# Ordering the hand-over from attention to expert tiles: weight copies as DMAs, a second bank, and moved steps in the last group

## The reference

```
h = layernorm(x) * (1 + ca) + sa
q, k, v = split(h @ w_qkv.T)                 # 8 heads of 16
qp, kp = elu(q @ proj) + 1, elu(k @ proj) + 1   # 128 features a head
out = qp (kp^T v) / (qp . sum kp)            # in blocks of 32 tokens
x = x + ga * (out @ w_out.T + b_out)
h = layernorm(x) * (1 + cb) + sb
gates = softmax(h @ w_red @ wg_n.T); pick the largest of 8 experts
y = gelu(h @ w1[e] + b1[e]) @ w2[e] + b2[e]  # 128 -> 512 -> 128
x = x + gb * y * gates[e]
```

## Time and profile before

| | us |
|---|---|
| median of 3 runs | 273.75 (273.18 to 275.33) |
| the profiled execution | 273.41 |
| its span in the profile | 271.7 |
| TensorE's mean granted clock | 0.992 of full |

### The profile page before, as it was taken

The page is one execution under the profiler, slowest core; times in us unless marked ns, Lnnn a source line. Parts: engine busy times, 40 slices in busy tenths (PEclk is TensorE's granted clock), DMA queues, the critical chain, the costliest instruction groups (busy, mean ns, idle before and its releaser), DMA issues.

```text
span 271.7 us, 11509 instructions
## 1 busy us (share of the span) xinstructions
PE 246.3 (91%) x4004; PEld 182.2 (67%) x4005; DVE 223.6 (82%) x743; ACT 182.3 (67%) x479; POOL 159.2 (59%) x199
## 2 busy tenths in 40 slices
PE   7699889999999999999999887997788999999960
PEld 3354555666766757667666565777678999999950
DVE  6778899999999999999999999687974776667640
ACT  2865657787687777868777655758866766766730
POOL 4423135174188487595771857786889974455550
PEclk9999999999999999999999999999999999999996
DMA  6910001955407218031040044222466444344300
GB/s 174 259 45 2 2 4 43 307 114 155 127 33 209 82 53 250 17 102 62 2 149 16 12 154 128 110 87 80 160 185 182 131 131 132 117 113 124 114 21 0
DMA packets 21583, 28.44 MB, mean 105 GB/s; under 512 B 3343, under 2 KB 16531, under 8 KB 21536
## 3 DMA queue, kind: packets, MB, share of 16 engines
q1 hardware_dynamic: 17920, 19.26, 25.7%
q0 software_dynamic: 3296, 8.41, 8.7%
q10 hardware_dynamic: 320, 0.13, 0.2%
HBM read 15.38 MB, written 10.64 MB: 96 GB/s over the span
## 4 chain that ended last, share of the span: by engine, by line
PE 56%; DVE 13%; issue 7%; POOL 7%; DMA 3%; SPq 1%; ACT 1%; POOLq 1%; DVEq 0%; ACTq 0%
PE ps L883 14%; PE ps L956 9%; PE ps L984 8%; PE ps L847 6%; PE ps L894 6%; DVE phi L1259 5%; PE ps L908 3%; PE ps L923 2%; POOL sorted_rows L504 2%; DMA rin<-sorted_rows 2%; PE ps L916 2%; PE ps L950 2%; PE ps L935 1%; PE ps L836 1%; POOL out L569 1%
## 5 line engine op out<-in xcount | busy, mean ns | idle before, releaser
L639 ACT ACTIVATE ebuf<-ps 128x512 f32<-128x512 f32 x128 | 69.5, 595 | 29.8 <-PE ps L883 29.5
L1259 DVE SCALAR_TENSOR_TENSOR phi<-ebuf,ps 128x512 f32<-128x512 f32 x128 | 81.1, 675 | 2.6 <-ACT ebuf L639 2.5
L883 PE MATMUL ps<-qk,proj_w 64*128 64x512 f32 x384 | 62.0, 427 | 4.9 <-DVE phi L1259 4.3
L701 ACT ACTIVATE gT<-ps,b_cols 128x128 f32<-128x128 f32 x156 | 44.6, 368 | 17.1 <-PE ps L956 13.9
L984 PE MATMUL ps<-w_sb,gT 128*128 x312 | 42.2, 278 | 4.2 <-DVE y L1553 2.8
L984 PEld LDWEIGHTS ps<-w_sb,gT 128*128 128x128 f32 x312 | 37.9, 192 | 6.1 <-issue 5.9
L883 PEld LDWEIGHTS ps<-qk,proj_w 64*128 64x128 f32 x384 | 31.2, 184 | 15.8 <-issue 4.1
L569 POOL DMA_INDIRECT out<-yo,tok x27 | 27.4, 1013 | 21.5 <-DVE yo L1569 19.0
L504 POOL DMA_INDIRECT sorted_rows<-rec,pos x32 | 32.8, 1024 | 8.5 <-issue 7.5
L894 PEld LDWEIGHTS ps<-phi 128*32 128x32 f32 x2048 | 22.5, 112 | 20.4 <-issue 13.5
L894 PE MATMUL ps<-phi 128*32 128x32 f32 x2048 | 29.6, 199 | 0.2 <-ACT a_sb L652 0.2
(11 more groups left out here) (205 smaller groups left out, 421.6 us busy)
## 6 DMA issues: line engine op xcount, KB each, us to landing
rin<-sorted_rows SPq DMA_DIRECT2D x39, 192.5 KB
vbd<-vals SPq DMA_DIRECT2D x32, 68.0 KB
w1b<-in_L_ffn_w SPq DMA_DIRECT2D x4, 512.0 KB
w_sb<-in_L_ffn_w SPq DMA_DIRECT2D x8, 256.0 KB
sorted_rows<-pad_rec SPq DMA_DIRECT2D x9, 192.5 KB, 6.0
x_all<-in_L_attn_x SPq DMA_DIRECT2D x2, 256.0 KB, 3.5
w1b<-in_L_ffn_b SPq DMA_DIRECT2D x1, 512.0 KB
sorted_rows<-rec,pos POOLq DMA_INDIRECT x32, 2.9
```

What stands on the lines that cost most here:

```text
L639: nc.scalar.activation(ebuf[:, h % 2, j, :], x_ps[h % 2][:, j, :], ACT.Exp, scale=1.0 / SHRINK, bias=math.log(SHRINK) - 1.0).then_inc(s_ex ...
L701: last = nc.scalar.activation(gT[:, b, c_, :], h_ps[b][:, j, i * P:(i + 1) * P], ACT.Gelu, bias=b1_cols[:, bass.ds(e * FC + c_, 1)])
L883: last = mm(x_ps[h % 2][:, j, :], proj_w[rows, w_part, h, :], qk_of(g, part, h // HT)[rows, :], start=w_part < part, stop=w_part == part)
L1259: last = v.scalar_tensor_tensor(out=phi[:, h % 4, j, :], in0=ebuf[:, h % 2, j, :], scalar=SHRINK, in1=x_ps[h % 2][:, j, :], op0=ALU.min, o ...
```

## The change

- SP copies the weights of all 12 early slots by DMA within on-chip memory (`load_weights`), instead of POOL (4) and ACT (8). Each has its own semaphore `f_we[s]`, for which `hidden` and `add_bias` wait. The first two go ahead of the row fetches, those of 2 to 5 between them, those of 6 to 11 after them, behind a wait for the last scores.
- The early slots' second layer shared one bank (4); from slot 5 (`Y_APART`) it alternates between banks 4 and 6, and `outer(s)` then waits for the bias of slot s - 2, no longer of s - 1.
- In DVE's last step, `score_sum(5)`, `score_inverse(5)`, `norm2_stats(6)` and `norm2_moments(6)` leave their place before the last `features` and come into `last_head`.
- POOL: `norm2_inverse(6)` goes behind the residual base and the first scatter of group 5; two more of these scatters come ahead of `norm2_scale(6)`, and all four ahead of `norm2_inverse(7)`.
- PE: the scores of group 7 come ahead of the first early slot; slot 2's first and slot 1's second layer go behind `turn_h2(6)`; `outer(2)` goes ahead of `rank(6)`. The fillers go from 12 to 4.
- ACT: the copies go; `gate_exp(7)` comes ahead of `build_scale(6)`, and `gate_exp(6)` ahead of `keep_h2T(7)`.
- DVE: `add_bias(2)` goes ahead of the positions of group 6, the score of group 7 behind its positions, `scale_add(3)` and `add_bias(4)` ahead of two operations of the full table.

```diff
 SP
-            sp.wait_ge(s_early, 1)
+            def load_weights(s):
+                e = sp.value_load(exp_i[0:1, s:s + 1], min_val=0, max_val=E - 1)
+                sp.dma_start(w_early[s], w1b2[:, bass.ds(e * (F + D), F + D)]).then_inc(f_we[s], 16)
+            sp.wait_ge(s_early, 2)
...
+            sp.wait_ge(s_xb, NG - 1)
+            for s in range(2):
+                load_weights(s)
             rows = [row_of(s) for s in range(RING)]
             for i in range(RECS):
                 sp.wait_ge(s_scat[i], 16 * TG * ((EARLY_G - i + RECS - 1) // RECS))
-            for s, row in enumerate(rows):
-                fetch(s, row)
+            fetch(0, rows[0])
+            fetch(1, rows[1])
+            for s in range(2, RING):
+                load_weights(s)
+                fetch(s, rows[s])
+            sp.wait_ge(s_a, H * NG)
+            for s in range(RING, EARLY):
+                load_weights(s)
 POOL
-                    for s in range(POOL_TAKES):
-                        take_early(s)
...
-                if prev:
+                if prev and not is_last(g):
                     norm2_inverse(g - 1)
...
             residual_base(NG - 1, False)
             scatter(NG - 3, [0])
+            norm2_inverse(NG - 2)
+            scatter(NG - 3, [1])
             apart()
-            scatter(NG - 3, [1])
+            scatter(NG - 3, [2])
             norm2_scale(NG - 2, False)
+            scatter(NG - 3, [3])
             norm2_inverse(NG - 1)
-            scatter(NG - 3, [2])
-            scatter(NG - 3, [3])
             apart()
             put_early(0)
 ACT
             keep_in(4, 4)
+            gate_exp(NG - 2)
             keep_h2T(NG - 1)
-            gate_exp(NG - 2)
             gelu(3, 1)
             keep_logits(NG - 1)
+            gate_exp(NG - 1)
             build_scale(NG - 2)
-            take_early(6)
-            gate_exp(NG - 1)
             keep_in(5, 5)
 PE (outer)
-                if isinstance(s, int) and s <= EARLY:
+                if shares_y(s):
                     if s > 0:
                         pe.wait_ge(f_s, s)
                 else:
                     pe.wait_ge(f_s, s - 1)
+                if isinstance(s, int) and s == Y_APART:
+                    pe.wait_ge(s_lgs, NG)
 PE (order)
-            keep_busy(3, t_ps)
+            keep_busy(2, t_ps)
+            scores(NG - 1, H - 2)
+            keep_busy(2, t_ps)
+            apply_values(NG - 1, 0, False)
+            scores(NG - 1, H - 1)
             slot_in(0)
-            scores(NG - 1, H - 2)
-            apply_values(NG - 1, 0, False)
+            apply_values(NG - 1, 1, False)
             slot_hidden(0)
             slot_in(1)
...
             slot_hidden(1)
-            apply_values(NG - 1, 1, False)
+            project_out(NG - 1, ps[:, 6, :])
             slot_in(2)
             slot_outer(0)
-            project_out(NG - 1, ps[:, 6, :])
+            pe.wait_ge(s_on, 2 * NG)
+            turn_h2(NG - 2)
             slot_hidden(2)
             slot_in(3)
             slot_outer(1)
-            turn_h2(NG - 2)
+            gate(NG - 2)
             slot_hidden(3)
-            gate(NG - 2)
             slot_in(4)
...
             turn_h2(NG - 1, ps[:, 6, :])
+            outer(2, 2, e_2)
             pe.wait_ge(s_lgs, NG - 1)
             rank(NG - 2)
             gate(NG - 1, ps[:, 6, :])
-            outer(2, 2, e_2)
 DVE (last_head)
+                score_sum(NG - 3)
                 position_rows(NG - 3)
+                score_inverse(NG - 3, False)
...
                 normalise_out(NG - 1, 0)
+                norm2_stats(NG - 2)
                 normalise_sum(NG - 1, 1)
+                norm2_moments(NG - 2)
                 normalise_inverse(NG - 1, 1)
 DVE (after the groups)
             scale_add(1, 1, 0)
+            add_bias(2, 2)
             position_rows(NG - 2)
...
-            add_bias(2, 2)
             route_max(NG - 1)
             route_below(NG - 1)
             route_first(NG - 1)
-            score_sum(NG - 1)
-            score_inverse(NG - 1, False)
             scale_add(2, 2, 0)
             add_bias(3, 3)
...
             position_out(NG - 1)
+            score_sum(NG - 1)
+            score_inverse(NG - 1, False)
```

More of the change, by code:

```diff
@@ L59, in adaln_kernel @@
     EARLY_TILES = EARLY_G * TG
+    Y_APART = 5
     WHOLE = SLOTS // RING * RING
@@ L244, in s_bank, with y_bank, shares_y @@
             return ps[:, 5 if s_early or b % 2 == 0 else 7, 0:P]
-        def y_bank(s_early, b):
-            return ps[:, 4 if s_early or b % 2 == 0 else 6, 0:D]
+        def y_bank(shares, b):
+            return ps[:, 4 if shares or b % 2 == 0 else 6, 0:D]
+        def shares_y(s):
+            return isinstance(s, int) and s < Y_APART
         m_ps = ps[:, 7, :]
@@ L279, in adaln_kernel @@
         f_in = [sem(f"f_in{b}") for b in range(RING)]
-        f_t = sem("f_t"); f_table = sem("f_table"); f_ts = sem("f_ts"); f_w = sem("f_w"); f_wa = sem("f_wa"); f_wp = sem("f_wp"); s_apart = sem("s_apart"); f_m = sem("f_m"); f_oa = sem("f_oa"); s_early = sem("s_early"); s_th = sem("s_th"); f_h = sem("f_h"); f_g = sem("f_g")
+        f_we = [sem(f"f_we{i}") for i in range(EARLY)]
+        f_t = sem("f_t"); f_table = sem("f_table"); f_ts = sem("f_ts"); f_w = sem("f_w"); s_apart = sem("s_apart"); f_m = sem("f_m"); f_oa = sem("f_oa"); s_early = sem("s_early"); s_th = sem("s_th"); f_h = sem("f_h"); f_g = sem("f_g")
         f_y = sem("f_y"); f_yd = sem("f_yd");
@@ L756, in _ @@
             keep_a(NG - 1, H - 2, False)
+            nc.scalar.activation(warm[:, :], neg_half[:, 0:1], ACT.Gelu).then_inc(f_table, 1)
+            keep_a(NG - 1, H - 1, False)
             act.wait_ge(s_early, 2)
@@ L759, in _ @@
             keep_in(0, 0)
[L760 removed]
             keep_in(1, 1)
[L762 removed]
             gelu(0, 0)
[L764 to L766 removed]
             keep_in(2, 2)
             gelu(1, 1)
[L769 removed]
+            keep_h2T(NG - 2)
             keep_in(3, 3)
[L771 removed]
             gelu(2, 0)
@@ L960, in hidden @@
             def hidden(s, b):
-                if isinstance(s, int) and s < POOL_TAKES:
-                    pe.wait_ge(f_wp, s + 1)
-                elif isinstance(s, int) and s < EARLY:
-                    pe.wait_ge(f_wa, s + 1 - POOL_TAKES)
+                if isinstance(s, int) and s < EARLY:
+                    pe.wait_ge(f_we[s], 16)
                 else:
@@ L975, in outer @@
             def outer(s, b, e):
-                early = isinstance(s, int) and s < EARLY
-                if isinstance(s, int) and s <= EARLY:
+                if shares_y(s):
                     if s > 0:
@@ L981, in outer @@
                     pe.wait_ge(f_s, s - 1)
+                if isinstance(s, int) and s == Y_APART:
+                    pe.wait_ge(s_lgs, NG)
                 pe.wait_ge(f_g, s + 1)
                 for c_ in range(FC):
-                    last = mm(y_bank(early, b), gT[:, b % 2, c_, :], w2_sb[:, bass.ds(e * (FC * D) + c_ * D, D)],
+                    last = mm(y_bank(shares_y(s), b), gT[:, b % 2, c_, :], w2_sb[:, bass.ds(e * (FC * D) + c_ * D, D)],
                               start=(c_ == 0), stop=(c_ == FC - 1))
@@ L1499, in step @@
                         residual(g - 1)
-                    if h == 6:
+                    if h == 6 and not is_last(g):
                         if prev2:
@@ L1544, in add_bias @@
                 early = isinstance(s, int) and s < EARLY
-                if early and s < POOL_TAKES:
-                    dve.wait_ge(f_wp, s + 1)
-                elif early:
-                    dve.wait_ge(f_wa, s + 1 - POOL_TAKES)
+                if early:
+                    dve.wait_ge(f_we[s], 16)
                 else:
@@ L1552, in add_bias @@
                 w = w_early[s] if early else w_slot[b]
-                v.tensor_tensor(y1[:, b % 2, :], y_bank(early, b), w[:, F:F + D], ALU.add).then_inc(f_s, 1)
+                v.tensor_tensor(y1[:, b % 2, :], y_bank(shares_y(s), b), w[:, F:F + D], ALU.add).then_inc(f_s, 1)
             def scale_add(s, b, k):
@@ L1573, in finish @@
                 scale_add(s, b, k)
-            add_bias(0, 0)
             residual(NG - 1)
             norm2_stats(NG - 1)
+            add_bias(0, 0)
             norm2_moments(NG - 1)
@@ L1608, in _ @@
             v.tensor_scalar(last_row[:, 0:E], carry[:, :], -float(P), None, ALU.add).then_inc(s_last, 1)
+            scale_add(3, 3, 0)
+            add_bias(4, 4)
             dve.wait_ge(s_tab, 1)
@@ L1613, in _ @@
             v.tensor_reduce(nt[:, :], full[:, :, :], AX.X, ALU.add).then_inc(s_tab, 1)
-            scale_add(3, 3, 0)
-            add_bias(4, 4)
             dve.wait_ge(s_tab, 3)
```

38 lines of the change are left out of this document (5 added, 33 removed).

## The result

The changed kernel takes **278.95 us** (median of 4 executions, 278.75 to 283.32; the record lists a fifth, of 278.10) against 273.75: a ratio of **1.0171, 95% interval 1.0125 to 1.0217**. It is slower, as forecast, but 3 us beyond the 276.0 and 0.75 us above the range's upper end of 278.2.

The account below looks back on a forecast made before the run. Slot 12's start bounds the change, where PE's list and the scatter-to-fetch line nearly tie. Terms 0.6 + 1.5 + 0.7 = 2.8, less 0.2 = 2.6, on 273.41 give 276.0 us; range 272.8 to 278.2.

Parts of the forecast that it names:

- the line: Chain through POOL's scatters and SP's row fetch to slot 12's start: 2.6 us later, fetch landing at 207.8.
- Parts 1 to 5: From SP's weight copies to `build_scale(6)`: fetch 0 at 170.2, h2(6) +0.6, positions +2.1, `build_scale(6)` +2.6 us.
- the tie: On POOL: its inverse waits for DVE's `norm2_moments(6)` at 172.1, just when it comes.
- Part 3: POOL's order: `norm2_scale(6)` behind one more scatter and an inverse; h2(6) at 178.8, +0.6; h2(7) +1.4 us.
- ACT's step: On ACT, `gate_exp(7)` ahead of `build_scale(6)`, which can start 0.7 us behind the score instead of 0.03: +0.6.
- the rule: Slot 12 starts 18.8 us after `build_scale(6)` ends, or when PE is free.
- Part 6: Second bank, ACT's loop and full table bring 0; last fetch lands at 207.8, PE idles some 3.4 us before it.
- rival C: Clock falls to half behind PE's idle before slot 12, 2 us more per slot: 278.5 to 280; chance 0.08.
- A: Not slower: POOL passes its scatters in no time that counts, fetch 0 lands by 169.2: 273.4 us; chance 0.15.
- B: Weights before rows: fetch 0 lands 1 us later, values, moments and POOL's list with it: 277.0 us; chance 0.17.
- D: Faster outright: slot 12 at PE's limit, `build_scale(6)` at 185.0: 272.5 to 270.5 us; chance 0.05.
- The rule on ring order: DMA engines consume one issuer's descriptors in ring order, so row fetches issued behind weight copies would wait for them.

Follow-up runs that it names:

- second profile: The changed kernel, unedited, profiled again in an execution of 280.02 us; that run's median 279.70 us, ratio 1.0206.
- first profile: The changed kernel, unedited, in its first measurement; the profiled execution was the longest, 283.32 us, and left out of the ratio.
- first set: Changed kernel unedited (279.70 us), with fillers in two idle times (277.64), POOL's order undone (278.01), ACT's order undone (279.81), fillers ahead of slot 12 alone (278.35).
- a1: Changed kernel with 11 fillers ahead of `turn_h2(6)` and 12 ahead of slot 12: 277.64 us, ratio 1.0107.
- b1: Changed kernel with 12 fillers ahead of slot 12 only: 278.35 us, ratio 1.0116.
- b0: Changed kernel with POOL's and ACT's order repaired, 4 fillers ahead of `turn_h2(6)` and 12 ahead of slot 12: 275.41 us, ratio 1.0025.
- g0: Changed kernel with 11 fillers ahead of `turn_h2(6)`, 12 ahead of slot 12 and 6 in the setup wait: 276.52 us, ratio 1.0073.
- c0: Kernel before with the weight copies by SP's DMAs only, nothing else moved: 278.18 us, ratio 1.0125.

## Why the prediction was right, and where it was wrong

The sum gave 276.0 us, and 278.95 was measured. The steps of the line, forecast against the second profile aligned:

| us | before | forecast | measured |
|---|---|---|---|
| fetch 0 lands | 167.7 | 170.2 | 170.5 |
| values (7, 1) end | 172.9 | 171.2 | 171.5 |
| `norm2_scale(6)` starts | 175.8 | 176.4 | 176.6 |
| h2(6) ready | 178.2 | 178.8 | 179.0 |
| `norm2_inverse(7)` ends | 179.6 | 181.4 | 181.8 |
| positions of group 6 start | 183.1 | 185.25 | 185.2 |
| score of group 6 ready | 185.2 | 187.35 | 187.3 |
| `build_scale(6)` ends | 186.5 | 189.15 to 189.35 | 189.0 |
| slot 12 starts | 205.3 | 207.8 | 207.9 |
| from there to the end | 66.4 | 66.4 | 67.8 (69.1 in the first profile) |

**Parts 1 to 5 held.** No step is off by more than 0.4 us. Fetch 0 is 0.3 late because SP issued it at 168.2 aligned and not at 167.7: a weight copy with its register load took SP 1.3 us and not 1.05. POOL waited 0.33 us for DVE's moments, the tie that Part 3 named. No `hidden` waited for weights. Part 3's claim, that what PE and DVE gain by their earlier start is spent on POOL because `norm2_scale(6)` stands behind one more scatter and an inverse, is shown from two sides: POOL has no idle time before `norm2_scale(6)`, and undoing POOL's order alone brings h2(6) forward by 1.6 and slot 12 by 1.4. ACT's step, +0.6, measured 0.49 when undone. From `build_scale(6)` to slot 12 were 18.9 us where the rule said 18.8; in the profiles of the first set it was 18.8 to 18.9 in every one.

**Part 6 and the sum failed in one term.** "PE idles some 3.4 us before it" was right (3.19), and the late slots were then taken as unchanged. They weren't: 1.4 us longer in one profile and 2.7 in the other, all of it blocks at half clock behind that idle time. In the first profile alone the idle time before `turn_h2(6)` cost too: slot 12 came at 209.24 aligned, 1.35 behind the second profile's. **The failed step is that Part 6 puts the 3.4 us of idle before slot 12 at their length alone and the clock behind them at nothing; that is rival C's condition, given 0.08.** What the runs show in its place: in all four profiles with an idle time of 2.25 us or more at slot 12 the clock fell behind it and the stretch to the end was 1.4 to 2.7 us longer; in the four with fillers ahead of slot 12 (a1, b1, b0, g0) it held, and that stretch was 65.9 to 66.4 us, as before. I read from the earlier trace rows that the granted clock first shows a fall 4.6 us after the last matmul, took idle times of about 3 us as safe, and gave the rival 0.08. That one row is a single instance, of a kernel's end. It shows that a fall came by then, not that none comes earlier. The same reading let me put down the eight fillers that go as time saved in PE's list, and never ask what they were doing next to an idle time. C's own time, 278.5 to 280, holds the medians of both measurements, 278.95 and 279.70. Its price, 2 us for each slot until the clock rises, was of the right size for one slot.

The Trainium skill (TensorE: Matmul & The Clock Gate, Part 1) says that the clock halves when PE has been idle, and that what the chip watches runs free of the kernel, so that one kernel differs from execution to execution. The traces here agree that PE was idle ahead of most falls and that executions differ: the same 1.48 us wait with the clock held in one profile and at 0.52 in another. Why they differ no run here shows. For the setup's fall this makes it a matter of chance in each execution.

**The rest, in numbers.** With fillers in all three places the excess is 0.73%, or 2.0 us of 274.5 by the ratio and 2.8 by the shortest executions; without them 1.71% and 2.06% in two measurements, 4.7 and 5.6 us. The 2.0 flatters the changed kernel, which has the setup's fillers there while the kernel before has not. By their own measurement (0.9972) they are worth about 0.8 us, so like for like the excess is 2.8. So the line has about 2.8 us, near the 2.6 summed, and the clock in the hand-over some 2 to 3. The difference of the changed kernel's medians with and without fillers comes from two chips; it is the weakest number here, and the profiles carry the argument, not it.

**The other rivals.** A (not slower) is out: POOL's scatters hold it, at about 1 us each. B's price was seen in one execution (the 4.36 us fetch). It wasn't the median's cause, since fetch 0 landed at 170.5 to 170.9 aligned in the seven other profiles of the changed kernel's order on SP and PE. D is out. The rule on ring order that the prediction weighed was not put to the test: in the second profile the two copies were issued at 162.4 and 163.7 aligned and landed 3.1 and 4.0 us later, ahead of fetch 0's issue at 168.2, and so it was in c0 and g0. Fetch 0 took 2.28 to 2.67 us in c0 and in these seven profiles, about as it did without them (2.47).

**What stays open.** Why a given idle time drops the clock in one execution and not in the next; which part of the 1.4 us of POOL's order is the scatter and which the inverse; what the other 0.7 us of the line are made of; what delayed the one fetch of 4.36 us; and whether the early scores and values (PE's new order) would bring something with the DMA copies left out.

## What to carry to other kernels

An idle time of TensorE in front of a long dense stretch has two prices, its length and what the clock takes behind it; price the second from the profile as soon as a change leaves PE waiting 2 us or more (shorter waits had it too here, in some executions), and look for the fillers that the change removes next to it. When work moves to the engine that issues DMAs, ask what stands behind it in that engine's list and what stands behind its consumer: two of the twelve copies ahead of the first fetch cost 1.25%, and with all of them, and five register loads, behind it no cost is left to see. A serial engine that feeds another (POOL here) should issue what others wait for ahead of what nobody waits for yet; half the loss on the line was scatters in front of a multiply and an inverse.

## What was not expected of the hardware

Of ten idle times of PE between 2.25 and 3.51 us in these profiles the granted clock fell behind seven and held behind three (2.26, 2.83 and 2.90 us). It also fell behind the one of about 1.5 us at 35 us in 8 of 13 profiles (0.52 to 0.71, where the kernel before held 1.00), and behind 0.90 to 0.92 us at 160 us in three (0.68 to 0.70), while it held behind the waits of 1.3 to 1.7 us before slot 0 in seven profiles. Length alone doesn't tell. A fall's price, read off the stretch behind slot 12, was 1.4 to 2.7 us in the four profiles that had one. An indirect scatter of 128 records holds POOL for 1.0 us, and the first fetch of a slot's rows takes 2.3 to 3.0 us from issue to landing, once 4.36. A copy of 328 KB with an address from a register costs SP 0.5 to 0.6 us to issue, 1.3 us from the start of one to the start of the next with the register's load, and lands 3.1 to 4.0 us after its issue.
